# Out-projection ahead of the time scan, in channel layout, in a one-layer language-model tower

## The reference, cut to what matters

```python
h = take(weight, x) * take(keep_mask, x)                       # 32 x 512 x 256
n = layernorm(h)
x_and_res = n @ in_proj_w.T                                    # 512 channels u, 256 channels res
u   = depthwise_conv4(u) + conv_b                              # causal, over time
g   = u * sigmoid(softplus(u @ dt_proj_w.T + dt_proj_b))
y_t = 0.9 * y_(t-1) + 0.1 * g_t                                # scan over the 512 tokens
h   = h + y @ out_proj_w.T + res                               # 512 -> 256 channels
q   = mx_quantise(layernorm(h)); wq = mx_quantise(ffn_w)       # blocks of 32, FP6 grid
h   = h + q @ wq.T + ffn_b
```

## Time and profile before

| | |
|---|---|
| median of 3 runs | 1170.4 us (1169.04 to 1170.95) |
| span of the profiled execution | 1167.3 us, first to last instruction |
| median less span | 3.1 us |
| VectorE busy | 1104.0 us, 95% |
| TensorE busy | 1011.5 us, 87% |
| GpSimd busy | 740.2 us, 63% |
| ScalarE busy | 582.0 us, 50% |

### The profile page before, as it was taken

One profiled execution on the slowest core, in us unless ns is written; L12 is line 12 of the kernel. 1 busy time (PEld: TensorE's weight loads), 2 busy tenths in 40 slices (PEclk: granted clock), 3 DMA queues, 4 the chain that ended last, 5 costly groups with the idle time before them and its releaser, 6 DMA issues.

```text
span 1167.3 us, 16219 instructions
## 1 busy us (share of the span) xinstructions
PE 1011.5 (87%) x5652; PEld 871.8 (75%) x5652; DVE 1104.0 (95%) x1627; ACT 582.0 (50%) x966; POOL 740.2 (63%) x521
## 2 busy tenths in 40 slices
PE   3789888889888889888889888899888899888887
PEld 2678777778777778777778777788777787777777
DVE  6879999999999999999999999999999999999995
ACT  4455445455445555444555454555454554454541
POOL 5556666676656676666676566676666675666562
PEclk9799999899989999998999899999989998999998
DMA  4001121112121112121211121211211121211111
GB/s 131 19 19 52 58 73 55 55 55 70 58 72 49 59 54 65 61 72 36 72 54 63 63 67 41 69 57 58 68 59 49 54 72 54 73 55 55 43 49 54
DMA packets 51470, 68.32 MB, mean 59 GB/s; under 512 B 10096, under 2 KB 42736, under 8 KB 51440
## 3 DMA queue, kind: packets, MB, share of 16 engines
q1 hardware_dynamic: 45296, 51.08, 13.4%
q0 software_dynamic: 6144, 16.85, 5.4%
HBM read 35.40 MB, written 32.51 MB: 58 GB/s over the span
## 4 chain that ended last, share of the span: by engine, by line
PE 73%; DVE 15%; issue 10%; ACT 1%; POOL 1%; DMA 0%; DVEq 0%; ACTq 0%; POOLq 0%
PE psZ L960 9%; PE psZ L961 9%; PE psZ L967 9%; PE psU L918 7%; PE psU L914 5%; PE psU L915 5%; PE psO L940 3%; PE psO L941 3%; PE psO L942 3%; DVE nT_lo L811 3%; DVE u L649 3%; PE psO L932 3%; PE psT L1027 2%; PE psO L934 2%; PE psO L1015 2%
## 5 line engine op out<-in xcount | busy, mean ns | idle before, releaser
L649 DVE SCALAR_TENSOR_TENSOR u<-psU,cw,u 128x511 f32<-128x511 f32 x378 | 265.2, 740 | 16.2 <-ACT u L436 11.7
L350 POOL TENSOR_TENSOR y_lo<-y,y_hi 128x512 fp32r<-128x512 f32 x128 | 163.2, 1287 | 180.8 <-ACT y_hi L456 180.1
L357 POOL TENSOR_TENSOR u_lo<-u,u_hi 128x512 fp32r<-128x512 f32 x128 | 189.9, 1483 | 115.5 <-ACT u_hi L443 107.2
L744 DVE TENSOR_TENSOR_SCAN y<-decay,g 128x512 f32<-128x512 f32 x128 | 231.2, 1806 | 3.4
L918 PE MATMUL psU<-nT_lo,in_hi 128*128 128x512 f32 x252 | 127.2, 505 | 121.1 <-DVE nT_lo L811 121.1
L960 PE MATMUL psZ<-u_hi,dt_hi 128*128 128x512 f32 x512 | 203.7, 398 | 4.9 <-ACT u_hi L443 4.4
L961 PE MATMUL psZ<-u_hi,dt_lo 128*128 128x512 f32 x512 | 202.9, 396 | 0.0
L967 PE MATMUL psZ<-u_lo,dt_hi 128*128 128x512 f32 x512 | 197.6, 397 | 0.0
L335 POOL DMA_INDIRECT rows<-table,ids x128 | 149.9, 1171 | 35.3 <-issue 34.1
L918 PEld LDWEIGHTS psU<-nT_lo,in_hi 128*128 128x128 f32 x252 | 60.1, 238 | 149.2 <-DVE nT_lo L811 135.3
L436 ACT ACTIVATE u<-psU,cb,cw 128x512 f32<-128x512 f32 x126 | 97.7, 775 | 145.0 <-PE psU L918 145.0
(11 more groups left out here) (109 smaller groups left out, 2489.0 us busy)
## 6 DMA issues: line engine op xcount, KB each, us to landing
out<-h SPq DMA_DIRECT2D x31, 512.0 KB, 2.9
turned<-xb SPq DMA_DIRECT2D x30, 512.0 KB, 2.7
xT<-turned SPq DMA_DIRECT2D x120, 128.0 KB, 2.9
rows<-table,ids POOLq DMA_INDIRECT x128
y<-dt_wT SPq DMA_DIRECT2D x1, 1024.0 KB, 5.8
g<-in_wT SPq DMA_DIRECT2D x1, 768.0 KB
ids<-x SPq DMA_DIRECT2D x32, 2.0 KB, 2.6
ow_stage<-out_wT SPq DMA_DIRECT2D x1, 512.0 KB, 7.8
```

The source lines that it names most:

```text
L350: pool.tensor_tensor(y_lo[:, m, :], y[:, m, :], f32(y_hi[:, m, :]), ALU.subtract).then_inc(y_lo_ready[m], 1)
L357: pool.tensor_tensor(u_lo[:, m, :], u[:, m, :], f32(u_hi[:, m, :]), ALU.subtract).then_inc(u_lo_ready[m], 1)
L649: dve.scalar_tensor_tensor(u[:, m, back:T], u_psum_tile(st, m)[:, 0:T - back], cw[:, m, TAPS - 1 - back:TAPS - back], u[:, m, back:T], ALU ...
L744: dve.tensor_tensor_scan(y[:, m, :], decay[:], g[:, m, :], 0.0, ALU.mult, ALU.add).then_inc(y_ready[m], 1)
```

## The change

The four blocks of the gated g are split into hi and lo in place of y. `out_proj(d)` makes the out-projection with output channels on partitions, 12 matmuls of 512 columns for each of two blocks of 128 channels, into `psY`, which is the tensor `psT` under another name. The scan runs on its two blocks, from PSUM to `scanned`. `merge(half)` turns `scanned` back to tokens by transposing matmuls into `psO`, and the residual products accumulate onto that. tanh is written over its own input in `psZ`, and the gate reads it there. The mean terms are formed on GpSimd, of a negated mean that VectorE leaves (`nm1`, `nm2`). The orders of all queues are new; ids are loaded and rows gathered earlier in the step. The dt weights get their own staging buffer, and the ffn weight is turned in `psO`.

The order of the calls in a step that is not near either end, before (-) and after (+); t is a call for the sequence of s-2, b for s-1, f for s+1:

```
-GpSimd: b split_y(3); split_u(0, 1); t bias; split_u(2, 3); b rstd2; f rstd1; t xT_lo; gather s+2; split_y(0, 1, 2)
+GpSimd: b split_g(3); gather s+2; split_u(0, 1, 2, 3); t bias; f rstd1, nmr1; split_g(0, 1); t xT_lo; b rstd2, nmr2; split_g(2)
-ScalarE: first_tap(0); b split_y(3); first_tap(1); split_u(0, 1); first_tap(2, 3); f mask_rows; split_u(2, 3); tanh(0); t split_xT; tanh(1); b normalise2; f normalise1; tanh(2); split_y(0); f split_nT; split_y(1); tanh(3); split_y(2)
+ScalarE: b split_g(3); f mask_rows; first_tap(0, 1); split_u(0, 1); first_tap(2, 3); split_u(2, 3); tanh(0, 1); f normalise1; split_g(0, 1); t split_xT; tanh(2); f split_nT; split_g(2); b normalise2; tanh(3)
-VectorE: convolve(0, 1); t dequantise, xb; convolve(2, 3); b add_h, statistics2, variance2; f statistics1; b mean_term2; f variance1; gate(0), scan(0); f mean_term1; gate(1), scan(1); b quantise; gate(2), scan(2); f split_nT; gate(3); t add_linear; scan(3)
+VectorE: convolve(0, 1); b scan(0); convolve(2, 3); t dequantise, xb; b scan(1); f statistics1, variance1; gate(0), gate(1); b add_h, statistics2, variance2; gate(2); f split_nT; b quantise; gate(3); t add_linear
-TensorE: in_proj(0, 1); b out_proj(0); in_proj(2, 3); b out_proj(1); dt_proj(0, 1); dt_proj(2); dt_proj(3); f transpose n1; t linear
+TensorE: in_proj(0, 1); b out_proj(0); in_proj(2, 3); b out_proj(1); dt_proj(0, 1); b merge(0, 1); dt_proj(2); f transpose n1; dt_proj(3); t linear
-SP: t turned, xT; wait for the gathers of s, load ids of s+2; t store
+SP: t turned, xT; wait for the gathers of s+1, load ids of s+3; t store
```

GpSimd (the gather's waits on the ids and on `h2_ready[1]` of the step before now stand ahead of split_g(3)):

```diff
+        g_hi, g_lo = sb("g_hi", [P, M, T], F32R), sb("g_lo", [P, M, T], F32R)
+        scanned = sb("scanned", [P, KD, T])
         h2 = sb("h2", [P, 2, C, D])
...
+        psY = psT
...
                     pool.tensor_tensor(rstd1[:], ve1[:], neg_half[:], ALU.pow).then_inc(rstd1_ready, 1)
+                    pool.wait_ge(rstd1_ready, s + 2)
+                    pool.tensor_tensor(nmr1[:], nm1[:], rstd1[:], ALU.mult).then_inc(nmr1_ready, 1)
+                def inverse_root2(part):
+                    cs = span(part)
+                    pool.wait_ge(var2_ready, s + (part or 0))
+                    pool.tensor_tensor(rstd2[:, cs], ve2[:, cs], neg_half[:, cs],
+                                       ALU.pow).then_inc(rstd2_ready, 1)
+                    pool.wait_ge(rstd2_ready, s + (part or 0))
+                    pool.tensor_tensor(nmr2[:, cs], nm2[:, cs], rstd2[:, cs], ALU.mult).then_inc(nmr2_ready, 1)
```

ScalarE:

```diff
                 def tanh(m):
                     act.wait_ge(z_psum[m], s + 1)
-                    if later(s):
-                        act.wait_ge(y_ready[m], s)
-                    act.activation(g[:, m, :], psZ[:, m % 2, :], ACT.Tanh, bias=gate_b[:, m:m + 1],
+                    act.activation(psZ[:, m % 2, :], psZ[:, m % 2, :], ACT.Tanh, bias=gate_b[:, m:m + 1],
                                    scale=0.5).then_inc(tanh_ready[m], 1)
-                def split_y(m, s=s):
-                    act.wait_ge(y_ready[m], s + 1)
+                def split_g(m, s=s):
+                    act.wait_ge(gated[m], s + 1)
                     if m == 0 and later(s):
                         act.wait_ge(o_psum[1], s)
-                    act.activation(y_hi[:, m, :], y[:, m, :], ACT.Copy).then_inc(y_hi_ready[m], 1)
```

VectorE (`variance1` and `variance2` each get a `tensor_scalar(nm, mean, -1.0)`):

```diff
                 def gate(m):
                     dve.wait_ge(tanh_ready[m], s + 1)
-                    dve.scalar_tensor_tensor(g[:, m, :], g[:, m, :], 3.0, u[:, m, :], ALU.add,
+                    if later(s):
+                        dve.wait_ge(g_lo_ready[m], s)
+                    dve.scalar_tensor_tensor(g[:, m, :], psZ[:, m % 2, :], 3.0, u[:, m, :], ALU.add,
                                              ALU.mult).then_inc(gated[m], 1)
-                def scan(m):
-                    dve.wait_ge(gated[m], s + 1)
-                    if later(s):
-                        dve.wait_ge(y_lo_ready[m], s)
-                    dve.tensor_tensor_scan(y[:, m, :], decay[:], g[:, m, :], 0.0, ALU.mult,
-                                           ALU.add).then_inc(y_ready[m], 1)
+                def scan(d):
+                    dve.wait_ge(o_psum[d], s)
+                    if later(s - 1):
+                        dve.wait_ge(m_psum[1], s - 1)
+                    dve.tensor_tensor_scan(scanned[:, d, :], decay[:], psY[:, d, :], 0.0, ALU.mult,
+                                           ALU.add).then_inc(scan_ready[d], 1)
```

TensorE:

```diff
-                def out_proj(half):
-                    if half == 0 and later(s - 2):
-                        pe.wait_ge(result_ready, s - 2)
+                def out_proj(d):
+                    if later(s - 1):
+                        pe.wait_ge(scan_ready[d], s - 1)
+                    o = slice(d * P, (d + 1) * P)
+                    for k in range(M):
+                        if d == 0:
+                            pe.wait_ge(g_hi_ready[k], s)
+                        pe.matmul(psY[:, d, :], ow_hi[:, k, o], g_hi[:, k, :], start=(k == 0), stop=False)
+                        pe.matmul(psY[:, d, :], ow_lo[:, k, o], g_hi[:, k, :], start=False, stop=False)
+                        if d == 0:
+                            pe.wait_ge(g_lo_ready[k], s)
+                        ins = pe.matmul(psY[:, d, :], ow_hi[:, k, o], g_lo[:, k, :], start=False,
+                                        stop=(k == M - 1))
+                    ins.then_inc(o_psum[d], 1)
+                def merge(half):
+                    if half == 0:
+                        if later(s - 2):
+                            pe.wait_ge(result_ready, s - 2)
+                        if st.second:
+                            pe.wait_ge(ffn_lo_ready, 1)
+                        for d in range(KD):
+                            pe.wait_ge(scan_ready[d], s)
                     chunks = range(C)[span(half)]
                     r = slice(DI, DI + D)
                     for c in chunks:
                         t = slice(c * P, (c + 1) * P)
-                        for k in range(KD):
-                            pe.matmul(psO[:, c, :], nT_hi[:, nb, k, t], in_hi[:, k, r],
-                                      start=(k == 0 and c == chunks[0]), stop=False)
-                            pe.matmul(psO[:, c, :], nT_hi[:, nb, k, t], in_lo[:, k, r], start=False, stop=False)
-                            pe.matmul(psO[:, c, :], nT_lo[:, nb, k, t], in_hi[:, k, r], start=False, stop=False)
-                        for k in range(M - 1):
-                            if c == 0:
-                                pe.wait_ge(y_hi_ready[k], s)
-                                pe.wait_ge(y_lo_ready[k], s)
-                            pe.matmul(psO[:, c, :], y_hi[:, k, t], ow_hi[:, k, :], start=False, stop=False)
-                            pe.matmul(psO[:, c, :], y_hi[:, k, t], ow_lo[:, k, :], start=False, stop=False)
-                            pe.matmul(psO[:, c, :], y_lo[:, k, t], ow_hi[:, k, :], start=False, stop=False)
-                    k = M - 1
-                    if half == 0:
-                        pe.wait_ge(y_hi_ready[k], s)
-                        pe.wait_ge(y_lo_ready[k], s)
+                        for d in range(KD):
+                            pe.matmul(psO[:, c, d * P:(d + 1) * P], scanned[:, d, t], ident[:],
+                                      start=(c == chunks[0] and d == 0), stop=False, is_transpose=True)
                     for c in chunks:
                         t = slice(c * P, (c + 1) * P)
-                        pe.matmul(psO[:, c, :], y_hi[:, k, t], ow_hi[:, k, :], start=False, stop=False)
-                        pe.matmul(psO[:, c, :], y_hi[:, k, t], ow_lo[:, k, :], start=False, stop=False)
-                        ins = pe.matmul(psO[:, c, :], y_lo[:, k, t], ow_hi[:, k, :], start=False,
-                                        stop=(c == chunks[-1]))
-                    ins.then_inc(o_psum[half], 1)
+                        for k in range(KD):
+                            pe.matmul(psO[:, c, :], nT_hi[:, nb, k, t], in_hi[:, k, r], start=False, stop=False)
+                            pe.matmul(psO[:, c, :], nT_hi[:, nb, k, t], in_lo[:, k, r], start=False, stop=False)
+                            ins = pe.matmul(psO[:, c, :], nT_lo[:, nb, k, t], in_hi[:, k, r], start=False,
+                                            stop=(c == chunks[-1] and k == KD - 1))
+                    ins.then_inc(m_psum[half], 1)
...
                 def dt_bank_free(m):
                     if m >= 2:
-                        pe.wait_ge(tanh_ready[m - 2], s + 1)
+                        pe.wait_ge(gated[m - 2], s + 1)
                     elif later(s):
-                        pe.wait_ge(tanh_ready[m + 2], s)
...
+                    for k in range(M - 1):
                         dt_hi_products(0, k)
-                        if st.first or k == M - 1:
-                            dt_hi_products(1, k if st.first else 0)
                         dt_lo_product(0, k)
```

(81 more changed lines are left out.)

150 lines of the change are left out of this document (68 added, 82 removed).

## The result

The changed kernel takes **1231.05 us** (median of 4, 1229.65 to 1232.29) against 1170.68: a ratio of 1.0515, 95% interval 1.050 to 1.053. It is slower; 1222 was forecast, in a range of 1183 to 1262.

What follows compares the result with a forecast made beforehand. VectorE's load bound the old kernel; afterwards queue order would set a 36.8 us step. 1167.3 + 30 x (36.8 - 35.12) + 1 = 1218.7 us, with the span 3.1 below the median: 1222 us, range 1183 to 1262.

Steps and rivals of the forecast that it cites:

- (b): VectorE from the second convolution: xd, xb, scan(1) at b + 7.28, statistics at 8.5; variance out at 10.7.
- (a): TensorE idles 3.6 us for u of block 0, then in_proj(2), first_tap(2); second convolution at 5.7, or 6.8 at the lower level.
- (c): First layernorm: GpSimd's power and product end at 12.05, ScalarE's normalise1 runs 12.1 to 14.1, then splits and xT.
- (d): GpSimd's queue: g_lo(0, 1), xT_lo to 19.9, only then second power and product to 21.2; 5.1 us of unneeded conversions ahead.
- (e): normalise2 21.25 to 23.35, then VectorE quantises to 26.4 and gate(3), queued behind, ends at 27.15.
- (f): ScalarE's split of g(3), mask_rows, then first_tap(0) 29.3 to 30.1; next convolution at b + 30.1.
- Rival B: Same loop without TensorE's lower clock level: step 35.8 us, 1192 us in all; chance 0.18.
- Rivals C and E: Dearer small GpSimd products (1273) or PSUM scan (1258); or one-PSUM-input gates or scans still wait for GpSimd (1258); chance 0.17 together.
- Rival D: Shorter loop, TensorE's load sets a 33 us step: 1108 us; decides once 1.7 us leave the chain; chance 0.15.
- The sum: Whole run: 1167.3 + 30 x (36.8 - 35.12) + 1 = 1218.7 us for the profiled execution.
- head and tail: Run's ends: nT_lo leaves up to 4.5 us earlier, last step's end grows; +1 us in all, bounds -4 and +9.
- one SBUF input is safe: VectorE beside GpSimd: instructions with two SBUF inputs wait; those with one, like the convolution's 4.24 us for six, do not.

Runs made afterwards that it cites:

- e2: Changed kernel with 12 extra, unread 512-column matmuls on TensorE between out_proj(0) and in_proj(2): 1173.1 us, ratio 1.0021.
- e3: Changed kernel with the second layernorm's power and product put ahead of xT_lo on GpSimd: 1104.8 us, ratio 0.9442.
- e4: Changed kernel with ScalarE's mask_rows moved from ahead of first_tap(0) back to behind first_tap(3): 1159.4 us, ratio 0.9901.
- e5: Changed kernel with tanh(3) ahead of normalise2 on ScalarE and gate(3) ahead of quantise on VectorE: 1142.9 us, ratio 0.9763.
- e1: Changed kernel with out_proj(1) put ahead of in_proj(2, 3) on TensorE, same matmuls in another order: 1174.6 us, ratio 1.0027.
- c1: Changed kernel with the reorderings of e3 and e5 together: 1084.4 us, ratio 0.9257.
- c3: c2 with the linear's addition put behind the next step's first convolution on VectorE: 1072.7 us, ratio 0.9159.
- b1: Kernel before the change with only the mean terms made as GpSimd products of a negated mean: 1159.4 us, ratio 0.9899.
- b2: Kernel before the change with only tanh written over psZ and the gates reading it there: 1151.5 us, ratio 0.9831.
- b3: Kernel before the change with b1 and b2 together: 1089.9 us, ratio 0.9302.
- c2: c1 with in_proj(0, 1) of the next sequence put ahead of the linear on TensorE: 1112.3 us, ratio 0.9500.

## Why the prediction was right

It was right in direction and in mechanism, and near in size: 60.4 us were added where 51 were forecast. One term of the loop was too small, and the mean over 30 steps hides it by luck. Here is the loop, point by point; all from (b) on is counted from the second convolution's start, b:

| | forecast | measured |
|---|---|---|
| (a) second convolution starts | 6.8 | 6.69 |
| (b) scan(1) | b + 7.28 | 8.37 |
| (c) normalise1 starts | b + 12.1 | 13.05 |
| (d) xT_lo ends | b + 19.9 | 20.62 |
| (d) second product ends | b + 21.2 | 21.87 |
| (e) gate(3) ends | b + 27.15 | 27.77 |
| (f) next convolution | b + 30.1 | 30.74 |
| step | 36.9 | 37.43; mean of the last 28: 37.28 |

- **(a) is the term that was too small.** TensorE waits 3.20 us (3.6 forecast) and the low level follows. The forecast let it end with first_tap(2), after six matmuls, and took 1.1 us for it. It held for all twelve, so that block 3's turn came 1.03 us late, and that is the excess at (b). e2 prices the level at 2.0 us per step. In four steps it ended sooner, and they take 36.0 to 36.5.
- **(b) to (f)**: each link after scan(1) took within 0.25 us of its forecast: 2.39 us for xT_lo (2.60 forecast), 0.20 for the product and 0.28 with its wait (0.2 and 0.3), 1.20 for the scan (1.28), 0.68 for the gate (0.74). Every link of (c) to (f) stands in the trace's chain in the order given. e3, e4 and e5 took one link each out, and each time the step got shorter.
- **Rival B**, the full level: 1192 was its price; e2 and e1 hold the level up behind this wait and come to 1173 and 1175. It did not happen here, but those runs show that it would have been worth more than I gave it, by 17 to 19 us: 1.0 us per step was reckoned, 2.0 is measured.
- **Rivals C and E** fell by rows: the 64 scans take 1.18 to 1.22 us, the 128 gates 0.68 to 0.69, the product 0.20.
- **Rival D** was right on what decides. It named the order behind xT_lo, and 1.7 us as the point where it turns; e3 takes 2.4 us out there and lands at 1104.8, 3 us from D's 1108. That nearness is partly luck: D's 33 us held 2 for the low level, which e3 does not have, and c1 and c3 with the same work on TensorE come to 32.2 and 31.87, so that in e3 TensorE's load did not yet set the step.
- D's estimate by the Trainium skill (TensorE: Matmul & The Clock Gate, Part 4), about 275 ns for a transpose: a single one lasts 272 ns here, so the figure agrees as a duration, but four are issued in 0.35 us, and sixteen at the issue rates seen (8 in 0.85, 4 in 0.35) cost TensorE 1.6 us of a step, not 4.4. By the page's figure D's step was 35.6; c3's is 31.87.
- **The sum.** The profiled span grew by 62.8 us, where the sum had 51.4. The 28 steps from the third nT_lo on grew by 2.13 us each, not 1.68: 59.6 us, 12.6 more than forecast. What came before grew shorter: nT_lo is 0.8 us earlier, and the two intervals behind it are 29.16 and 34.25 us instead of 33.45 and 35.95, so the head gave back 6.8 us (4.5 at most forecast). The end, from the last nT_lo, is 10.0 us longer (4 to 8 forecast); 2.2 of it are a wait of nm2, told below, the rest was not traced. So head and tail with those two intervals come to 3.2 us, where the sum had 4.4 (1 and twice 1.68). They are no part of the miss; the step is. The mean of all 30 intervals, 36.91, meets the forecast 36.8 only since the two short ones are in it.
- **From span to median.** The 3.1 us between the span and the median of the kernel before were taken over. In the runs of this case the time is 1.8 to 1.9 us above the span. So the profiled execution of the kernel before took about 1169.1 us, 1.3 below the median, and the changed kernel's took 1232.02, 1.0 above its own. The growth of the span is larger than that of the median by these 2.3 us, and the miss on the median is that much smaller, 9 us.

Where did VectorE's 7 us go? Into its waits: 4.16 for normalise2, 1.83 for first_tap(0), 1.27 and 1.03 for the second convolution. In all it is idle for 10.3 of 37.43 us, where it was for 0.8 of 35. Before, its load was the bound, so a cut counts (b1, b2). The change cut far more than that and gave the queues new orders, two of which lengthened the loop: the power of the second layernorm, which had stood ahead of xT_lo, and the masks, which had stood behind first_tap(3). e3 and e4 put these back. The third link, gate(3) behind the quantise, is as it was before; what it cost there was not tried.

Still open: why the same wait before in_proj(2), 2.25 us in e5 and 1.6 in e4, is followed by the low level in some steps and not in others. What the structural part is worth by itself, beside b3, was not tried with both orders set as well as can be; c3 is 17 us below b3.

## What to carry to other kernels

When a change takes the load off the fullest engine, walk once around the loop by queue order before believing the load: here the step grew by 2.1 us with 7 us less on VectorE, because of three links (a power behind a conversion and a tap behind the masks, both new, and a gate behind a quantise, which was there before). Price an idle piece of TensorE twice, for itself and for the matmuls at the lower level behind it, and look first at swaps that break it into pieces. When an instruction that had to wait for GpSimd is freed, look for the next one with two SBUF inputs: in b1 it inherited the wait. When an order is changed, look at what comes to lie beside the short instructions of the chain, as `bscale` in c1.

## What the runs showed that was not expected

- **The low level multiplies what an order saves.** e3 takes 2.4 us out of the chain and gives 4.2 per step; e4 takes 1.7 and gives 2.4. With a wait of TensorE before in_proj(2) of 3.2 us the low level came in every step, at 1.6 to 2.3 in two thirds of them or more (e4, e5, c2), and at 0.8 or less (e2, e3, c3) the clock from 300 to 900 us is 1.00. It is 1.00 in c1 too, where the one long wait, 1.7 us, is ahead of the linear.
- **Extra work made the kernel faster.** 2.8 us of matmuls that nobody reads save 58 us (e2).
- **A tensor_scalar with one SBUF input waits for GpSimd too.** The new nm2, 0.17 us in b1, takes 0.64 in the steady step, and 2.36 in the last one, where it stands on the chain; it ends with the conversion beside it, the last step's rows being:

```profile
1189.14 2.36 DVE L684 TENSOR_SCALAR nm<-mv 128x4 f32<-128x4 f32 x1
```

```profile
1189.08 2.38 POOL L404 TENSOR_TENSOR xT_lo<-xT,xT_hi 128x1024 fp32r<-128x1024 f32 x1 [2.00 <-ACT xT_hi L509]
```

So "one SBUF input is safe", as the prediction read it from the convolution, is too wide: some 2.2 us of the longer tail are this wait, and `bscale` in c1 is a second case. The prediction also gave the Trainium skill's rule (SBUF — State Buffer, "Who interferes with whom") without its exception: an instruction in a mode that uses both ports does contend, and tensor_scalar is named among those that can enter one. Both cases are tensor_scalar; that the mode is the reason no run here shows.
